# Weights staged and split while w2 streams, 13 RNN steps ahead of the LSTM, maxima from sums of squares

## The reference

```python
x = x + L0(x, cond)     # (x * ys) @ w0, scaled by d = rsqrt(ys^2 @ w0^2 + eps)
x = x + L1(x, cond)     # RNN: h = tanh(h @ Wh + x @ Wx + b), 128 steps, h0 = cond
x = x + L2(x, cond)     # x + x @ (base + A_b B_b^T); A_b, B_b (512 x 8) come from
                        #   gelu(layernorm(cond) @ w1 + b1) @ w2 + b2
x = x + L3(x, cond)     # LSTM, 128 steps, gates i, f, o, g of 512 each, h0 = cond
```

## Time and profile before

| | us |
|---|---|
| median of 3 runs (1275.09 to 1275.97) | 1275.89 |
| the profiled execution, its own time | 1275.62 |
| span of its trace, first to last instruction | 1273.8 |
| busy: PE / DVE / ACT / POOL | 1199.6 / 808.4 / 422.0 / 58.7 |
| share of the span: PE / DVE / ACT | 94% / 63% / 33% |

### The profile page before, as it was taken

How to read it: one execution, slowest core, us unless ns; L and a number is a source line. 1 busy time by engine, 2 the same in 40 slices (tenths; PEclk the granted TensorE clock), 3 DMA queues, 4 the chain that set the end, 5 groups by cost and what they waited for, 6 DMA issues and landing times.

```text
span 1273.8 us, 50351 instructions
## 1 busy us (share of the span) xinstructions
PE 1199.6 (94%) x22860; PEld 786.4 (62%) x22860; DVE 808.4 (63%) x2288; ACT 422.0 (33%) x1083; POOL 58.7 (5%) x84
## 2 busy tenths in 40 slices
PE   6777399999999999999999999999999999999997
PEld 4354166666666666666666666666666666666653
DVE  6487866666666666666666666666666666665543
ACT  3132333333333333333333333333333333333322
POOL 1000000000000000000000000000000000000000
PEclk9878699999999999999999999999999999999999
DMA  9785000000000000000000000000000000000000
GB/s 317 249 272 219 9 3 19 20 19 19 19 20 19 19 15 8 19 20 19 19 20 19 20 19 12 10 19 20 19 19 19 19 19 20 10 12 11 11 10 18
DMA packets 23719, 52.52 MB, mean 41 GB/s; under 512 B 2417, under 2 KB 2545, under 8 KB 22481
## 3 DMA queue, kind: packets, MB, share of 16 engines
q1 hardware_dynamic: 19184, 41.43, 9.1%
q10 hardware_dynamic: 4320, 7.87, 2.1%
HBM read 40.37 MB, written 8.39 MB: 38 GB/s over the span
## 4 chain that ended last, share of the span: by engine, by line
PE 69%; DVE 17%; ACT 7%; issue 5%; DMA 1%; SPq 0%; DVEq 0%; POOL 0%; POOLq 0%
PE ps_gates L939 21%; PE ps_gates L930 19%; PE ps_x L891 8%; PE ps_l L891 7%; PE ps_rnn L948 4%; PE ps_rnn L951 3%; ACT x L399 2%; PE ps_lstm_t L983 2%; PE ps_z L891 2%; DVE x1T L816 2%; PE ps_gates L867 2%; DVE x1T L812 1%; DVE shared L728 1%; ACT shared L453 1%; ACT rnn_h L399 1%
## 5 line engine op out<-in xcount | busy, mean ns | idle before, releaser
L930 PE MATMUL ps_gates<-wx_hi,x 128*32 128x512 f16 x4096 | 266.5, 380 | 20.6 <-DVE wx_lo L517 20.6
L939 PE MATMUL ps_gates<-wh_hi,lstm_h 128*32 128x512 f16 x4096 | 266.7, 380 | 3.2 <-ACT lstm_h L399 3.2
L930 PEld LDWEIGHTS ps_gates<-wx_hi,x 128*32 128x32 f16 x4096 | 109.7, 97 | 132.9 <-DVE wx_lo L517 20.8
L728 DVE SCALAR_TENSOR_TENSOR shared<-ps_gates,tile_un,b_sb 128x256 f32<-128x256 f32 x256 | 112.0, 479 | 100.1 <-PE ps_gates L939 100.1
L939 PEld LDWEIGHTS ps_gates<-wh_hi,lstm_h 128*32 128x32 f16 x4096 | 97.6, 96 | 99.1 <-ACT lstm_h L399 4.5
L453 ACT ACTIVATE shared<-shared 128x256 f32<-128x256 f32 x128 | 53.4, 417 | 309.0 <-DVE shared L728 309.0
L930 PE MATMUL ps_gates<-wx_lo,x 128*32 128x512 f16 x2048 | 133.6, 381 | 0.0
L939 PE MATMUL ps_gates<-wh_lo,lstm_h 128*32 128x512 f16 x2048 | 132.7, 379 | 0.0
L948 PEld LDWEIGHTS ps_rnn<-rnn_h,wh_hi 128*128 128x128 f16 x2048 | 91.1, 97 | 59.0 <-issue 53.1
L948 PE MATMUL ps_rnn<-rnn_h,wh_hi 128*128 128x64 f16 x2048 | 121.6, 193 | 5.6 <-DVE rnn_h L759 5.6
L951 PE MATMUL ps_rnn<-rnn_h,wh_lo 128*128 128x32 f16 x2048 | 116.7, 177 | 0.0
(11 more groups left out here) (185 smaller groups left out, 1742.1 us busy)
## 6 DMA issues: line engine op xcount, KB each, us to landing
ring<-in_hw SPq DMA_DIRECT2D x16, 1024.0 KB, 10.6
outT<-late SPq DMA_DIRECT2D x32, 256.0 KB, 2.1
xT_sb<-in_xT ACTq DMA_DIRECT2D x30, 256.0 KB, 2.8
wh_staged<-in_wh SPq DMA_DIRECT2D x4, 1024.0 KB, 12.8
ring<-in_wx SPq DMA_DIRECT2D x4, 1024.0 KB, 6.9
shared<-in_w SPq DMA_DIRECT2D x1, 1024.0 KB, 5.8
stage<-in_hw SPq DMA_DIRECT2D x1, 1024.0 KB, 8.0
shared<-in_wx SPq DMA_DIRECT2D x1, 1024.0 KB, 10.5
```

The costliest lines, as they stand in the source:

```text
L728: nc.vector.scalar_tensor_tensor(gates[:, half], ps_gates[t % 2][:, half], tile_un[:, a, 1:2], b3_sb[:, half], ALU.mult, ALU.add).then_inc ...
L930: last = nc.tensor.matmul(ps_gates[t % 2][B * j:B * j + B, :], x16[:, part, k, at:at + B], w[:, k, GW * j:GW * j + GW], start=(n == 0 and ...
L939: last = nc.tensor.matmul(ps_gates[t % 2][B * j:B * j + B, :], lstm_h16[:, part, k], w[:, k, GW * j:GW * j + GW], start=False, stop=(final ...
```

## The change

- The LSTM no longer starts after 8 RNN steps in rounds but after 13 (LEAD). The work is written in slots t = -13 to 127; slot t has LSTM step t where t >= 0. RNN steps 0 to 12 lie in slots -13 to -1, steps 13 to 127 in slots (r-13)*118//115, that is in slots 0 to 116 but for 39 and 78; slots 117 to 127 have none.
- L0 and L1 of tile c = r//4 + 1 are cut into halves, one for each RNN step: L0 beside r%4 = 0 and 1, L1 beside r%4 = 2 and 3. L2 of tile a+1 goes with the LSTM's slot: z and a quarter of base at t%4 = 0, two quarters at 1, a quarter and the low rank part at 2, nothing at 3. So the RNN's r%4 and the LSTM's t%4 are offset by 1 in slots 0 to 38, by 0 in slots 40 to 77, and by 3 in slots 79 to 116.
- In slots without an RNN step L2 stands before the transpose of lstm_h.
- x2 = x1 + h moves from VectorE to GpSimd, 128x128 each step.
- The maxima of w0, Wx, Wh, and of both LSTM weights are replaced by sums of squares: a Square with accumulation on ScalarE (its root is taken on the exponent).
- All weights have staging of their own; Wx and Wh of the LSTM load while w2 streams, and are squared, split high (ScalarE) and low (VectorE, in halves) in the 13 loading slots. `wx3_high(k)` waits for `wx3_low(k-1)`, likewise for Wh, since high k overwrites what low k-1 reads.
- b2 enters by one more fp32 matmul for each w2 piece; closing four pieces is now a ScalarE copy. The rows of B are moved by four fp32 matmuls instead of 16 DMAs.
- The scales of four tiles are made at once at the start; x has a ring of four buffers.

The pieces below are in order: the slots; ScalarE's squares, high halves and its part of a slot; VectorE's part of a slot, in the loading and then beside the LSTM; TensorE's b2 matmul and where the w2 pieces stand; GpSimd's part of a slot.

```diff
-LAG = 2
+LEAD = 13
+RNN_SPREAD = 118
+        slot_of = [r - LEAD if r < LEAD else (r - LEAD) * RNN_SPREAD // (T - LEAD) for r in range(T)]
...
+            def squares(out_, in_, column):
+                return nc.scalar.activation(out_, in_, ACT.Square, accum_out=absmax[:, column:column + 1]).then_inc(sq_ready, 1)
...
+            def wx3_high(k):
+                wait(act, wx3_lo_ready, k)
+                high(wx3_part(0, k), wx3_staged(k), s_wx3).then_inc(wx3_hi_ready, 1)
...
+                if r == 0:
+                    copy_rows(0)
+                if r is not None and r < KC:
+                    wx3_squares(r)
+                if r is not None and 3 <= r < 3 + KC:
+                    wx3_high(r - 3)
+                if r is not None and 4 <= r < 4 + KC:
+                    wh3_squares(r - 4)
+                if r == 7:
+                    copy_rows(1)
+                if r is not None and 8 <= r < 8 + KC:
+                    wh3_high(r - 8)
+                if r == 9:
+                    move_b()
...
+                    if 4 <= r < 4 + KC:
+                        wx3_low(r - 4, 0)
+                    if 9 <= r < 9 + KC:
+                        wh3_low(r - 9, 0)
+                    dve.wait_ge(rnn_hi_ready, r + 1)
+                    nc.vector.scalar_tensor_tensor(rnn_h16[:, :, 1], rnn_h[:], s_h, rnn_h16[:, :, 0],
+                                                   ALU.mult, ALU.subtract).then_inc(rnn_lo_ready, 1)
...
+                if t >= 0 and s == 0 and a + 1 < TILES:
+                    mask_z(a + 1)
+                    gate_scales(a + 1)
+                    zm_low(a + 1)
...
+                    if r % STEPS == 1 and c < TILES:
+                        x1(c)
...
+                if t >= 0 and s == 2 and a + 1 < TILES:
+                    x3(a + 1)
...
+                    if r % STEPS == 1 and c < TILES:
+                        x1_low(c)
+                    if r % STEPS == 3:
+                        if XT_RING <= c + 2 < TILES:
+                            tile_scales(c + 2, 1)
+                        if c + 1 < TILES:
+                            xs_low(c + 1)
+                        if c < TILES:
+                            xw1(c)
...
+                nc.tensor.matmul(ps_rows[q][B * j:B * j + B, :], ident[0:2 * RANK, at:at + 1].broadcast_to([2 * RANK, B]), b2_sb,
+                                 start=True, stop=False, tile_position=(0, B * j))
+            W2_AFTER = {0: (2, 3), 1: (4,), 3: (5,), 6: (6,), 7: (7,), 8: (8, 9), 9: (10,), 10: (11,), 11: (12, 13), 12: (14, 15)}
...
+                    nc.gpsimd.tensor_tensor(x2T[i % X2_RING][:, :, s], x1T[i % 2][:, :, s], rnn_h[:], ALU.add)\
+                      .then_inc(x2_ready, 1)
```

More of the change, by code:

```diff
@@ L24 @@
 X3_TOP = 2
-X2_RING = 8
+X2_RING = 5
+XT_RING = 4
 LN_EPS = 1e-5
@@ L124, in build @@
+        gates_ring = sb("gates_ring", [P, 2, GW])
+        gates_sb = [gates_ring[:, q] for q in range(2)]
+        unused16 = gates_ring[:].rearrange("p q n -> p (q n)").bitcast(fp16)
         late = sb("late", [P, KC * D])
@@ new lines, in x1_low, with xw1 @@
+            def x1_low(c):
+                dve.wait_ge(x1_hi_ready, c + 1)
+                low(x1_16[:, 1], x1T[c % 2][:].rearrange("p k t b -> p k (t b)"), tile_s[:, c, 1:2], x1_16[:, 0])\
+                    .then_inc(x1_lo_ready, 1)
+            def xw1(c):
+                dve.wait_ge(xw1_ps, c + 1)
+                nc.vector.scalar_tensor_tensor(xw1T[:].rearrange("p k t b -> p k (t b)"),
+                                               ps_l1[:].rearrange("p (k n) -> p k n", k=KC), tile_s[:, c, 4:5],
+                                               b1T_sb[:].unsqueeze(2).broadcast_to([P, KC, TOK]), ALU.mult, ALU.add)\
+                  .then_inc(xw1_ready, 1)
@@ new lines, in l2_weights @@
+                gate_scales(0)
+                for k in range(0, KC, 2):
+                    dve.wait_ge(base_hi_ready, k // 2 + 1)
+                    low(base_lo[:, k:k + 2].rearrange("p k n -> p (k n)"), late[:, D * k:D * k + 2 * D], s_base[:],
+                        base_hi[:, k:k + 2].rearrange("p k n -> p (k n)")).then_inc(base_lo_ready, 1)
+                dve.wait_ge(base_lo_ready, 2)
+                mask_z(0)
+                dve.wait_ge(b_hi_ready, 1)
+                low(b_lo[:], b_rows, s_b[:], b_hi[:]).then_inc(b_lo_ready, 1)
@@ L844, in _ @@
             last.then_inc(aeT_ps, 1)
+            pe.wait_ge(ys_ready, 2)
+            pe.wait_ge(sq_ready, 1)
+            for oc in range(KC):
+                for k in range(KC):
+                    last = nc.tensor.matmul(ps_x3[:, B * oc:B * oc + B], w0_sq[:, k, P * oc:P * oc + P], ysq[:, k],
+                                            start=(k == 0), stop=(k == KC - 1))
+            last.then_inc(dsum_ready, 1)
             pe.wait_ge(ld_w1, 16)
@@ L872, in _, with move_b @@
-            w2_piece(1)
-            W2_BETWEEN = {(-1, 0): (2, 3, 4), (-1, 1): (5, 6), (-1, 2): (7,), (0, 3): (8, 9, 10, 11)}
-            def l2_weights():
-                for n in range(RANK + 4, 2 * RANK):
-                    w2_piece(n)
+            def move_b():
+                pe.wait_ge(rows_ready, 2)
+                pe.wait_ge(half_ident_ready, 1)
+                for half in range(2):
+                    for q in range(2):
+                        at = BH * RH * q
+                        last = nc.tensor.matmul(ps_turned[half][at:at + BH * RH, :], half_ident[:, half], rows[:, q],
+                                                start=True, stop=True, tile_position=(0, at))
+                    last.then_inc(b_ps, 1)
```

1152 lines of the change are left out of this document (613 added, 539 removed).

## The result

The changed kernel takes **1314.74 us** (median of 4 runs, 1311.79 to 1318.07) against 1275.74 for the kernel before on the same chip: ratio 1.0307, 95% interval 1.0275 to 1.0340. It is slower, as forecast, but by 39 us where 9 were forecast, and outside the range.

What follows compares the result with a forecast made beforehand. PE was taken to bound the steady LSTM stage, with loading costed apart: LSTM start 160.5 plus stage 1123 gives a span of 1283.5, and with 1.8 for the run 1285 us; own range 1275 to 1294, full range 1261 to 1300.

Steps and rivals of the forecast that it cites:

- LSTM stage: From the LSTM's start to the end: 1098.5 us plus 24.6 of stalls, 1123, 7 more than before.
- The two losses in slots 0 to 38: VectorE's whole-tile work late for the next gates: 0.6 us lost at t%4 = 0, 1.45 at t%4 = 2.
- rival B: LSTM stage: no pile-ups, late VectorE slots hide behind PE; 20 us less, 1265; chance 0.14.
- with b2's matmul (two more instructions of eight) 2.94: Loading: price of one w2 piece on PE, 2.35 us without b2's matmul and 2.94 with it.
- step 8's L0: Loading: end of RNN steps 4 to 7, bound by a chain through ACT and DVE; L0 starts at some 102 us.
- The tail from the last piece: Loading, from the last w2 piece at 142 us to the LSTM's start at 160.5: 18.5 us.
- Wh's scale with GpSimd 4.4: Loading, RNN steps 4 to 7: 4.4 us for Wh's scale, an item beside the chain through ACT and DVE.
- from 0 to 0.2 us in each late slot: LSTM stage: GpSimd's add x2 = x1 + h slowing DVE, 0 to 4 us in all, 1 taken.
- Rival D: Loading: PE idle in r = 3 to 7 keeps the clock low; 4 pieces 12 us more, 1296; chance 0.11.
- Rival C: Loading: Square leaves the tanh table, eight squares with two table loads each; 15 us more, 1300; chance 0.07.
- Rival A: Loading is PE's: ACT and DVE overlap, r = 4 to 7 take 3.5 us each; start near 138, 1262; chance 0.14.
- the sum without pile-ups: LSTM stage added up part by part before VectorE's stalls: 1098.5 us, 17.5 below the 1116.0 before.

Runs made afterwards that it cites:

- the free slots first: Changed kernel with its two slots without an RNN step at LSTM slots 0 and 1 instead of 39 and 78: 1288.79 us, against 1314.74.
- the early pieces: Changed kernel with one b2 matmul for four pieces, w2 pieces moved into RNN steps 4 to 8, the free slots first: 1277.51 us.
- the fastest without added matmuls: Changed kernel with one b2 matmul for four pieces, w2 pieces moved earlier, the free slots first, x2 on VectorE throughout: 1261.53 us.

## Why the prediction missed

- **LSTM stage: right, in sum and in parts.** Forecast 1123, rounds of 37.1, 35.4 and 35.2; measured 1122.9, 37.0, 35.4, 35.1. The two losses in slots 0 to 38, forecast 0.6 and 1.45, measured 0.5 and 1.4. That the sum agrees to 0.1 us is in part luck: the 3.5 us of slots 39 and 40 were in no item, and other items were taken a little too high (0.4 a round in slots 40 to 77 where most lose 0.3, 1 us in slots 79 to 116 that does not show). That the two losses come from how the quarters stand to each other, and not from where in the kernel they lie, is shown by the free slots first: rival B was the gain of another schedule, not of this one.
- **The step that failed** is the price "with b2's matmul (two more instructions of eight) 2.94" for a w2 piece. It took 2.35 (7.12/3 is 2.37) from three pieces that overlap, put it on pieces with another matmul between them, and added a quarter. Measured: 4.52, 1.58 more, 25 us over 16 pieces. By the medians b2 costs 14.3 us in the changed kernel; some of the 25 lies beside other work. Of the 31.9 us by which the LSTM started late, 13.9 arose in RNN steps 8 to 12, where PE is the chain: eight pieces at 1.58 are 12.6 of them. Up to step 8's L0 17.7 had gathered (119.7 for 102; the forecast's own items add up to 103.4, not 102): 5.2 by the first product (44.2 for 39, of which two pieces are 3.2), 9.1 by the last square of Wx (71.1 for 62), and the rest behind it, where GpSimd's wait of 8.8 us stands on the chain. The tail from the last piece was right, 18.8 (18.5). The Trainium skill, page "TensorEngine Tiling (Array Packing)", section Key Properties, says that changing the tiling mode, as against the tile, drains TensorE. That a matmul of 16 rows among those of 128 is such a change is our reading; the trace agrees with it: with 16 rows nothing overlaps (9.04 us a pair), with 128 rows the same pair takes 7.1.
- **GpSimd was priced by its busy time alone** ("Wh's scale with GpSimd 4.4", the add "from 0 to 0.2 us in each late slot"). In the loading, its switches of 6 to 9 us are worth 10 us once b2 is out of the way (15 with the early pieces), and 1 while it is not. The idle time ahead of a row that was quoted held the number. The Trainium skill ("GPSIMD Engine Reference", section Instruction dispatch) gives about 6 us for the first call of a kernel newly loaded; the trace agrees in size, with 5.9 to 7.7 ahead of a reduction and 6.8 to 8.9 ahead of an add or product, but pays it at every change of kind. That these waits are such loads no run here shows.
- **Rival D, the low clock**: there (0.59 from 80 to 100, piece 6 at 7.4 us), forecast at 11 us, measured 2.9, at the edge of the noise, in the version where it could be lifted.
- **Rival C fell.** Square with accumulation takes 1.89 us for 128x2048 and 0.19 to read the sum, which overlap: 1.99 together, just the 1.99 taken, and it brings no table load. **Rival A fell too**: PE has 6.64 us of work in the 20 from 80 to 100. Only from 119.7 on is the loading PE's, as the forecast itself had it from step 8.
- **The account**: 1314.7, less 9.4 (b2 four times instead of 16), less 10.3 (GpSimd's adds), less 2.9 (clock), is 1292.1. The forecast was 1285 (its own terms give 1285.6). Of the 7 us between, up to 4.9 are the four b2 matmuls still in it (1300.45 without any against 1305.35), though the forecast's 2.94 had a share for b2 as well. The rest is open.

## What to carry to other kernels

Before a duration from a trace is multiplied, look whether it was of one thing alone or of neighbours that overlap, and what the change puts between them; a matmul of another height is enough to end it. For an engine that is seldom busy, read the idle time ahead of its operations with "issue", not only their lengths: an add of 0.45 us between two reductions stood between waits of up to 6.7 and 8.9. And when two causes cover each other, taking either away shows nothing (5.5 more and 1.1 less here): remove them together before calling one of them harmless.

## What was not expected of the hardware

- fp32 matmuls of 128 rows into neighbouring groups of 32 columns overlap: 16 instructions take 5.37 us, 8 alone 3.62; with a 16-row matmul ahead of each group of 8 there is no overlap at all (4.52 each).
- VectorE's low half of h is slow beside GpSimd's larger product, not beside the small add. Groups with mean ns of the changed kernel and of the fastest without added matmuls, which has the add on VectorE:

```profile
L928 DVE SCALAR_TENSOR_TENSOR rnn_h<-rnn_h,scales 128x128 f16<-128x128 f32 x128 | 76.3, 596 | 42.2 <-ACT rnn_h L444 39.5
```

```profile
L931 DVE SCALAR_TENSOR_TENSOR rnn_h<-rnn_h,scales 128x128 f16<-128x128 f32 x128 | 71.9, 562 | 45.6 <-ACT rnn_h L441 45.6
```

Before the change the mean was 0.35 us. Now three steps of four still have 0.35 to 0.36, and the one in which GpSimd multiplies x by ys (128x512) has 1.41, or 1.25 with the add on VectorE. Timelines of VectorE and of GpSimd in the changed kernel:

```profile
357.62 1.44 DVE L928 SCALAR_TENSOR_TENSOR rnn_h<-rnn_h,scales 128x128 f16<-128x128 f32 x1
```

```profile
357.23 0.46 POOL L418 TENSOR_TENSOR x_ring<-x1T,rnn_h 128x128 f32<-128x128 f32 x1 [8.84 <-ACT rnn_h L539]
357.64 1.27 POOL L399 TENSOR_TENSOR xsT<-xT_sb,ysT 128x512 f32<-128x512 f32 x1
```

The half ends 0.15 us behind the product. So the add beside it costs the low half 0.03 us in the mean (0.60 against 0.56), and VectorE is relieved of 0.28 us a step; that this makes no difference to the time is because PE bounds the stage, which takes 1098.4 us with the add on GpSimd and 1097.8 with it on VectorE, both times the sum without pile-ups.
